# Scores by query of the first two or three steps of the last three layers, and their maxima, moved into the MLP before

## What is computed

```python
x = L0(x, ctx)      # two cross attentions of 16 heads x 128, then MLP 0 (gelu)
x = L1(x, ctx)      # LN, cross attention of 16 heads x 16, then MLP 1 (LN, gelu)
x = L2(ctx, x)      # keys and values from [ctx, x] (512 keys), 16 heads x 16, then MLP 2 (rms)
x = L3(x, ctx)      # 32 query heads x 8 on 8 key heads, additive mask, layer norm at the end
# each attention: softmax(q k^T) v, so each query row needs the maximum of its 256 or 512 scores
```

## Time and profile before

| | us |
|---|---|
| median of three runs (1248.19 to 1248.85) | 1248.57 |
| the profiled execution | 1249.79 |
| its span, first to last instruction | 1248.4 |
| PE / PE weight load / DVE / ACT / POOL busy | 1203.5 / 1029.8 / 888.7 / 779.8 / 598.9 |
| handoff MLP 0 to layer 1, 1 to 2, 2 to 3 | at 695, 850 and 1052 |

### The profile page before, as it was taken

The page is one execution under the profiler, slowest core; times in us unless marked ns, Lnnn a source line. Parts: engine busy times, 40 slices in busy tenths (PEclk is TensorE's granted clock), DMA queues, the critical chain, the costliest instruction groups (busy, mean ns, idle before and its releaser), DMA issues.

```text
span 1248.4 us, 27144 instructions
## 1 busy us (share of the span) xinstructions
PE 1203.5 (96%) x9940; PEld 1029.8 (82%) x9940; DVE 888.7 (71%) x2304; ACT 779.8 (62%) x1889; POOL 598.9 (48%) x966
## 2 busy tenths in 40 slices
PE   8999999999999999999989899999999899999997
PEld 7999999999999999999978665786675577666664
DVE  5887877779887777778865787537788464666764
ACT  4876666668876566666874566645676654555553
POOL 3784555548875555454862443504444131324333
PEclk9999999999999999999999999999999999999999
DMA  5540100013431001001420220122222012121100
GB/s 170 153 141 31 35 26 27 27 39 107 142 100 35 27 26 35 27 27 28 126 74 27 81 81 28 51 69 74 84 68 70 10 60 64 54 70 42 40 12 18
DMA packets 56820, 75.03 MB, mean 60 GB/s; under 512 B 11312, under 2 KB 30576, under 8 KB 56688
## 3 DMA queue, kind: packets, MB, share of 16 engines
q1 hardware_dynamic: 51568, 72.75, 19.1%
q0 software_dynamic: 5120, 0.56, 0.3%
HBM read 49.46 MB, written 1.05 MB: 40 GB/s over the span
## 4 chain that ended last, share of the span: by engine, by line
PE 80%; DVE 7%; issue 5%; ACT 4%; POOL 2%; DMA 1%; ACTq 0%; DVEq 0%; POOLq 0%
PE bank L125 19%; PE bank L127 18%; PE bank L126 18%; PE bank L2052 5%; PE bank L771 4%; PE bank L1999 3%; PE bank L2009 3%; PE bank L1985 2%; PE bank L2010 2%; PE bank L1981 1%; ACT PT L2126 1%; DMA Q<-rows 1%; PE bank L178 1%; PE bank L713 1%; PE bank L1736 1%
## 5 line engine op out<-in xcount | busy, mean ns | idle before, releaser
L1095 POOL TENSOR_SCALAR E<-E,rl 128x256 f32<-128x256 f32 x256 | 243.6, 962 | 210.2 <-DVE rl L980 210.2
L2126 ACT ACTIVATE PT<-bank 128x512 f32<-128x512 f32 x320 | 173.5, 594 | 92.6 <-PE bank L2010 56.0
L846 ACT ACTIVATE QTh<-bank,bqs 128x256 fp32r<-128x256 f32 x128 | 60.8, 475 | 156.3 <-PE bank L127 156.2
L2207 DVE CUSTOM_DVE_ANT_0 Em<-bank,M 128x256 bf16<-128x256 f32 x256 | 95.1, 420 | 53.8 <-PE bank L1985 22.3
L856 ACT ACTIVATE E<-bank,nm 128x257 f32<-128x257 f32 x256 | 119.5, 481 | 1.2 <-DVE nm L950 1.0
L984 DVE TENSOR_TENSOR PTl<-bank,PTh 128x512 fp32r<-128x512 f32 x128 | 88.0, 688 | 27.3 <-ACT PTh L868 26.8
L957 DVE SCALAR_TENSOR_TENSOR QTl<-bank,bqs,QTh 128x256 fp32r<-128x256 f32 x128 | 61.6, 481 | 64.0 <-ACT KT L847 63.2
L868 ACT CAST PTh<-bank 128x512 fp32r<-128x512 f32 x128 | 75.2, 588 | 43.2 <-PE bank L771 43.2
L2201 DVE TENSOR_REDUCE nm<-bank 128x1 f32<-128x512 f32 x128 | 83.3, 685 | 23.5 <-PE bank L1981 22.3
L950 DVE TENSOR_REDUCE nm<-bank 128x1 f32<-128x257 f32 x256 | 95.5, 414 | 3.6 <-PE bank L127 3.6
L1999 PE MATMUL bank<-Q,K 51*128 51x256 f32 (+1 forms) x640 | 85.2, 315 | 4.9 <-DMA Q<-rows 2.4
(11 more groups left out here) (438 smaller groups left out, 4382.2 us busy)
## 6 DMA issues: line engine op xcount, KB each, us to landing
stage<-in_wts SPq DMA_DIRECT2D x99, 256.0 KB, 3.3
U<-in_vrows SPq DMA_DIRECT2D x64, 256.0 KB, 2.7
K<-stage SPq DMA_DIRECT2D x48, 128.0 KB
Q<-stage SPq DMA_DIRECT2D x48, 128.0 KB
K<-stage SPq DMA_DIRECT2D x48, 64.0 KB
Q<-stage SPq DMA_DIRECT2D x48, 64.0 KB
K<-xh SPq DMA_DIRECT2D x16, 128.0 KB, 3.0
Q<-rows POOLq DMA_DIRECT2D x96, 4.0 KB, 1.7
```

The costliest lines, as they stand in the source:

```text
L1095: m = pool.tensor_scalar(s.E[:, i % 3, t, 0:256], s.E[:, i % 3, t, 0:256], s.rl[:, r, t:t + 1], None, ALU.mult)
L2126: act.activation(s.PT[i % s.NPT][:, 2 * u:2 * u + 2, :].rearrange("p a b -> p (a b)"), s.STB[y][:], ACT.Exp).then_inc(S["t_ex"])
L2207: dve.tensor_tensor_reduce(out=s.Em[:, (2 * i + e) % 4], in0=bank[:, e * 256:e * 256 + 256], in1=s.M3[:, j, e, :], scale=-1.0, scalar=3.4e ...
```

## The change

Steps 0 and 1 of layer 1, and 0 to 2 of layers 2 and 3, have their scores by query and maxima formed in steps 14 and 15, or 13 to 15, of the MLP before, in banks 6, 3 and 4. Batch 0's preparation comes a step earlier, layer 2 turns and projects x in bank 6, the fillers stay in the later of the first five steps only, and one-off work moves: the ones of K on GpSimd from before step 0 to step 3, the Exp table from step 3 to step 0, the ones of Q and V on ScalarE from steps 0 to 6 to steps 3 to 8. The tiles nm and Em are taken before the MLP.

```diff
@@ mlp_pe, mlp_dve, in each step i
+        for n in nxt.early(i):
+            heads_early_pe(c, nxt, n)
...
+        for n in nxt.early(i):
+            for k in nxt.in_step(n):
+                heads_maxima(c, nxt, k)
@@ tables
-              8: ["stats"], 9: ["norm"], 10: ["turn", "scale"], 11: ["th", "tl", "res"], 12: ["q0", "q1", "qh", "ql"],
-              13: ["q_out", "stats+"], 14: ["norm+"], 16: ["turn+", "scale+"]},
+              8: ["stats"], 9: ["norm", "turn", "scale"], 10: ["th", "tl", "res"], 11: ["q0", "q1", "qh", "ql"],
+              12: ["q_out", "stats+"], 13: ["norm+"], 16: ["turn+", "scale+"]},
...
-              9: ["turn", "th", "tl", "res"], 10: ["q0", "q1", "qh", "ql"], 11: ["q_out", "x0", "x1", "xh", "xl"],
-              12: ["x_out", "v2", "v3", "vb"]},
+              8: ["turn", "th", "tl", "res"], 9: ["q0", "q1", "qh", "ql"], 10: ["q_out", "x0", "x1", "xh", "xl"],
+              11: ["x_out", "v2", "v3", "vb"]},
-          3: {3: ["mask"], 6: ["k0", "kh", "kl"], 7: ["v0", "v1", "va", "k_out"], 8: ["maskparts"],
-              9: ["turn", "th", "tl", "res"], 10: ["q0", "q1", "qh", "ql"], 11: ["q_out"]}}
+          3: {3: ["mask"], 6: ["k0", "kh", "kl"], 7: ["v0", "v1", "va", "k_out"],
+              8: ["turn", "th", "tl", "res"], 9: ["q0", "q1", "qh", "ql"], 10: ["q_out", "maskparts"]}}
+EARLY = {1: {14: 0, 15: 1}, 2: {13: 0, 14: 1, 15: 2}, 3: {13: 0, 14: 1, 15: 2}}
...
-ONES_AT = {1: {0: ("q", 1, 0), 1: ("q", 1, 1), 2: ("v", 1, 0), 4: ("q", 2, 0), 5: ("q", 2, 1), 6: ("v", 2, 0)},
-           2: {1: ("q", 1, 0), 2: ("q", 1, 1), 3: ("v", 1, 0), 4: ("v", 1, 1)}, 3: {1: ("v", 1, 0)}}
+ONES_AT = {1: {3: ("v", 1, 0), 4: ("q", 1, 0), 5: ("q", 1, 1), 6: ("q", 2, 0), 7: ("q", 2, 1), 8: ("v", 2, 0)},
+           2: {5: ("q", 1, 0), 6: ("q", 1, 1), 7: ("v", 1, 0), 8: ("v", 1, 1)}, 3: {5: ("v", 1, 0)}}
@@ class Heads
+        self.E, self.EB = len(EARLY[l]), [c.B[6], *c.B[3:5]]
...
+    def query_bank(self, n):
+        return self.EB[n % 3] if n < self.WD * self.E else self.SB[n % 3]
+    def asked(self, n):
+        return self.in_step(n) if n >= self.E else ()
@@ heads_by_query, now a function of its own
+    if n < 3:
+        w.wait_ge(S["m_hf"], 4 * (l - 1) + 3)
+        w.wait_ge(S["m_x"], 4 * (l - 1) + 2)
+    elif first <= n < first + 3:
+        w.wait_ge(S["m_gelu"], 16 * l)
+        w.wait_ge(S["t_mx"], s.o["mx"] + first * k)
+    else:
+        w.wait_ge(S["t_mx"], s.o["mx"] + (n - 2) * k)
@@ heads_pe: keep_busy
-        if n < s.L:
-
-            w.wait_ge(S["m_x"], 4 * (l - 1) + 2)
+        if s.E <= n < s.L:
+
+            w.wait_ge(S["t_mx"], s.o["mx"] + s.WD * s.E * (2 if l == 3 else 1))
             ones(s.STB[1], {1: 4, 2: 4, 3: 6}[l])
@@ heads_act
-        if n == s.L - 2:
+        if n == 0:
             w.wait_ge(S["neghalf"], 1)
             act.activation(c.tiny[:], c.neghalf, ACT.Exp)
@@ heads_pool
-    ones_keys(c, s, 1)
     for n in range(s.steps()):
         for g in s.turns_at(n - 1):
             maxima_rows(g)
+        if n == 3:
+            ones_keys(c, s, 1)
         for g in s.turns_at(n):
             maxima_parts(g)
```

More of the change, by code:

```diff
@@ L1257, in take_first @@
         self.qbs = sb("qbs", [128, 2], F32, self.above)
+        self.nm = self.main("nm", [128, 4, self.G, 2])
+        if self.l == 3:
+            self.Em = self.main("Em", [128, 4, 256], BF16)
     def take_rest(self, c):
@@ L1281, in x_bank, with early @@
     def x_bank(self, b):
-        return self.MB if b and self.l == 2 else self.PB
+        return self.PB if self.l != 2 else self.MB if b else self.EB[0]
+    def query_bank(self, n):
+        return self.EB[n % 3] if n < self.WD * self.E else self.SB[n % 3]
+    def early(self, i):
+        return [EARLY[self.l][i]] if i in EARLY[self.l] else []
+    def asked(self, n):
+        return self.in_step(n) if n >= self.E else ()
     def all(self, n):
@@ L1548, in heads_prep_pe @@
                 w.wait_ge(S["h_y"], s.pk(0) + 1)
+        elif l == 2:
+            w.wait_ge(S["m_hf"], 4 * (l - 1) + 3)
         else:
@@ L1955, in heads_sp, with heads_ready, heads_by_query, heads_early_pe @@
         w.wait_ge(S["st_out1"], 48)
+def heads_ready(c, s, b):
+    S, w, l = c.S, c.pe_w, s.l
+    for x in "qk":
+        w.wait_ge(S["dma_h" + x], 64 * s.spreads(b + 1))
+        w.wait_ge(S["dma_l" + x], 32 * s.spreads(b + 1))
+    if l == 2:
+        w.wait_ge(S["dma_hx"], 64 * (b + 1))
+        w.wait_ge(S["dma_lx"], 32 * (b + 1))
+    if l != 3:
+        w.wait_ge(S[f"dma_mask{b % 2}"], 32 * (2 * (l - 1) + b // 2 + 1))
+def heads_by_query(c, s, n, e):
+    S, pe, w, l = c.S, c.pe, c.pe_w, s.l
+    p, u, y = s.unit(n)
+    q, r = p % s.P, p // s.P % s.NR
+    at = s.at(q, y, s.R)
+    bank, first, k = s.query_bank(n), s.WD * s.E, 2 if l == 3 else 1
+    if n < 3:
+        w.wait_ge(S["m_hf"], 4 * (l - 1) + 3)
+        w.wait_ge(S["m_x"], 4 * (l - 1) + 2)
[4 more added lines that the diff above has]
+        w.wait_ge(S["t_mx"], s.o["mx"] + (n - 2) * k)
+    if l == 2:
+        pe.matmul(bank[:], s.Q[r][at, q, u * 128:u * 128 + 128], s.K[r][at, q, :], start=True, stop=True
+                  ).then_inc(S["t_s"])
+        return
+    z = pe.matmul(bank[:, 256 * e:256 * e + 256], s.Q[r][at, q // s.blocks, 128 * e:128 * e + 128],
+                  s.K[r][at, q // s.rp, :], start=True, stop=True)
+    if e == 1:
+        z.then_inc(S["t_s"])
+def heads_early_pe(c, s, n):
+    if n == 0:
+        heads_ready(c, s, 0)
+    for e in (range(1) if s.l == 2 else range(2)):
+        for k in s.in_step(n):
+            heads_by_query(c, s, k, e)
 def heads_pe(c, s, nxt):
@@ L1960, in heads_pe @@
     nh, nkt = s.nh, s.nkt
[L1962 to L1988, removed]
     def by_key(n, e):
@@ L2013, in fours @@
     def fours(n):
[L2015 to L2018, removed]
+        if 0 < n < s.T and n % s.TB == 0:
+            heads_ready(c, s, n // s.TB)
         for e in (range(1) if l == 2 else range(2)):
-            for k in s.in_step(n):
-                by_query(k, (e,))
+            for k in s.asked(n):
+                heads_by_query(c, s, k, e)
         for e in range(2):
@@ L2183, in heads_act, with heads_maxima @@
         close_act(c, s)
-def heads_dve(c, s, nxt):
[L2187 to L2209, removed]
+def heads_maxima(c, s, n):
+    S, dve, w, l = c.S, c.dve, c.dve_w, s.l
+    p, u, y = s.unit(n)
+    i = 2 * p + y
+    g, h = i // s.G, i % s.G
+    nm, bank = s.nm[:, g % 4, h, :], s.query_bank(n)
+    w.wait_ge(S["t_np"], s.o["g"] + g - 3)
+    w.wait_ge(S["t_s"], s.o["s"] + n + 1)
+    if l == 1:
+        dve.tensor_reduce(nm, bank[:].rearrange("p (a b) -> p a b", a=2), AX.X, ALU.max, negate=True
+                          ).then_inc(S["t_mx"])
+    elif l == 2:
+        dve.tensor_reduce(nm[:, u:u + 1], bank[:], AX.X, ALU.max, negate=True).then_inc(S["t_mx"])
+    else:
+        j = i // s.nh % 2
+        w.wait_ge(S[f"ld_m3{j}"], 16 * (i // s.nh // 2 + 1))
+        for e in range(2):
+            w.wait_ge(S["t_mx"], s.o["mx"] + 2 * i + e - 3)
+            dve.tensor_tensor_reduce(out=s.Em[:, (2 * i + e) % 4], in0=bank[:, e * 256:e * 256 + 256],
+                                     in1=s.M3[:, j, e, :], scale=-1.0, scalar=3.4e38, op0=ALU.add,
+                                     op1=ALU.min, accum_out=nm[:, e:e + 1]).then_inc(S["t_mx"])
@@ L2211, in heads_dve @@
+def heads_dve(c, s, nxt):
+    w, l = c.dve_w, s.l
     mlp_end(c, w, l - 1)
     for n in range(s.steps()):
-        for k in s.in_step(n)[:s.WD - 1]:
-            maxima(k)
+        for k in s.asked(n)[:s.WD - 1]:
+            heads_maxima(c, s, k)
         for b, x in s.preps(n - 1):
@@ L2223, in heads_dve @@
             piece_dve(c, k)
-        for k in s.in_step(n)[s.WD - 1:]:
-            maxima(k)
+        for k in s.asked(n)[s.WD - 1:]:
+            heads_maxima(c, s, k)
     if l == 3:
```

9 lines of the change are left out of this document (2 added, 7 removed).

## The result

| | before | after |
|---|---|---|
| median of the runs, us | 1248.71 (4 runs, 1248.19 to 1250.28) | 1260.1 (4 runs, 1257.87 to 1264.12) |
| ratio, 95% interval | 1 | 1.0088 [1.0076, 1.0100] |
| profiled execution / its span | 1249.79 / 1248.4 | 1261.03 / 1259.5 |
| granted clock, mean over the span | 0.990 | 0.980 |
| time at the lower clock in the profiled execution | 25.7 | 52.5 |

The change makes the kernel 0.9% slower, 11 us. The forecast had the sign, its 4.95 us were less than half of it, and 1260.1 lies above the range.

A forecast was written before the change was run, and what follows sets the result against it. TensorE was taken as the bound; layer 1 +0.8, layer 2 +1.7 and layer 3 +2.45 gave +4.95 us on a median of 1248.57, so 1253.5. The forecast's own range was 1250.5 to 1257.5; 1246.0 to 1257.0 leaves out under 2 in 10.

The forecast's parts named there:

- What bounds it: Whole kernel: TensorE is the bound, so a microsecond counts only if TensorE loses or saves it; moved waits count nothing.
- Layer 1: Handoff from MLP 0 and layer 1: late maxima and K's later fill against fillers gone, +0.8 us.
- (c): Layer 1: k of batch 1 still waits for residual and scale; layer 2: waits of 1.3 for residual, 1.3 for parts.
- rival 3: Handoff to layer 1: the clock falls there too, a low stretch of 3.4 us costs 1.7, 1255.2; chance 0.15.
- (d): Layer 1: later K fill delays step 8, +0.8 (-1.5 to +2.5); layer 2: casts in steps 5 to 8, +0.8.
- Layer 2: MLP 1 and layer 2: 0.9 for casts in the MLP, 0 up to step 5, 0.8 after it, +1.7 us.
- (a): Layer 2: two casts on ScalarE meet in one MLP step and delay gelu, +0.9 us, bounds 0 and 1.05.
- (b): Layer 2: early scores in MLP steps 13 to 15, with maxima between low parts on VectorE, +1.4 us.
- Layer 3: MLP 2 and layer 3: q0 0.25 later, and a gap of 4.1 us drops the clock, +2.2; +2.45 us.
- Rival 1: All three layers: fills of K and Exp table done before TensorE needs them, -3.2 us, 1245.4; chance 0.22.
- Rival 2: Whole kernel: waits come but the clock holds and casts in steps 5 to 8 are covered, +1.95, 1250.5; chance 0.21.
- Rival 4: MLPs: a late spread or maximum holds the early scores and TensorE, another 2 to 4 us, 1256.5; chance 0.04.

The follow-up runs named there:

- a1: Changed kernel with GpSimd's fill of K behind the first group's parts (layers 1, 3) or second group's (layer 2): 1258.67 us, 1.0071 to the kernel before.
- a4: Changed kernel with the Exp table loaded in step 3 again: 1257.85 us, 1.0063 to the kernel before.
- c4: b1 plus fillers dropped from the early steps: 1252.68 us, 1.0017 to the kernel before.
- a3: Changed kernel with the casts of ones on ScalarE back where they were: 1263.14 us, 1.0098 to the kernel before.
- d1: b1 plus the fill of K in step 3 and fillers only in steps 3 and 4: 1256.8 us, 1.0055 to the kernel before.
- c1: b2 with layer 2's fill of K cut into two halves, in steps 2 and 4: 1246.69 us, 0.9964 to the kernel before.
- c3: b1 plus the fill of K in step 3: 1254.19 us, 1.0032 to the kernel before.
- d2: b1 plus fillers only in steps 3 and 4 and the Exp table at step 0: 1258.43 us, 1.0058 to the kernel before.
- b1: Kernel before plus only early scores, their maxima and earlier preparation; fillers, casts, Exp table and fills of K unmoved: 1253.23 us, 1.0023 to the kernel before.
- b2: Changed kernel with all side edits rearranged: fill as in a1, Exp table in step 2, fillers numbered per step, casts spread: 1250.47 us, 1.0003 to the kernel before.
- a2: Changed kernel with the fillers of all five first steps back: 1256.2 us, 1.0059 to the kernel before.

## Why the prediction was wrong in size

**What bounds it: right.** TensorE is busy 176 of 184 us in layer 3 and 146.5 of 157 in layer 2, and of its waits 2.33 us (a1, layer 1) and 1.5 (a4, layer 3) came off where the work that they waited for was moved.

**Layer 1: the waits right, a fall of the clock missed, +0.8 in the sum, +2.6 measured** (720.68 against 717.40 at step 8, less the 0.69 that was there at the start). Normalised tokens, maxima before GL (+0.90 for +0.75) and k_out behind the fill came as forecast. Missed in (c) was a new fall of the clock: the fillers and scores that had stood in the gap ahead of k were only counted as filling, and without them the gap is 1.85 us and the clock low for 3.4 us. This is rival 3's event, and it came besides the forecast, not in its place. The Trainium skill (TensorE: Matmul & The Clock Gate, PE-mode transpose) says that transposes don't count as TensorE being busy in the way of other matmuls; the trace agrees with it only in so far as the clock fell, at 700.19, after a gap of 1.85 us with four transposes before it. That it was they is not shown: c4 has the same gap of 1.85 us and ran on at 1.00 from 697 to 704. In (d), q_out's issues ended at 718.2 for a forecast 716.3; the start, MLP 0 and that low stretch explain it. The wait of 2.33 us at step 8 came behind it, and the low stretch that begins at 713.8 (before: 712.3) lasts 10.2 us and not 6.8. The upper bound, +2.5, was near the measured value.

**Layer 2, (a), (b), (c): right.** MLP 1 +2.57 for 2.3, up to step 5 -1.41 for -1.4. **(d): the step that failed**, +0.8 for casts in steps 5 to 8, bounds 0 and 2.0, where +5.78 was measured from step 5 to the layer's end. Its price was that of ScalarE's work, and a fall of the clock was put at nothing. The clock is what costs most there, at 1.2 GHz for 13.7 us (4.9 of the 5.78), from 1.0 us behind the turn that had waited 1.37 us. For this gap, hardly longer than the 1.20 us of that in the earlier trace rows, the prediction counted 1.3 us in (c) and no fall, although it took the fall in layer 3 from that very row. In a3 and d1 the casts are gone from these steps and the low clock is not, for 10.2 us each; in c1, with casts of its own in steps 2 to 4 and 9, the wait is short (0.59 us) and the clock stays up. That the wait brings the fall is likely and not shown, since c3 waits 1.39 us and the clock stays up.

**Layer 3: right, by its sum** (2.45 for 2.44: MLP 2 +1.67, the rest +0.77). The gap is 4.13 for 4.1. The clock fell inside it, 1.7 us before its end, for 6.8 us: 5.1 at half clock behind the restart, where 4.4 were taken. The chain ahead of q0 was put at 3.25 us, though its five rows add up to 3.06 without any overlap; 3.24 were measured from the residual to q0, so part of that agreement is luck. What the table at step 0 costs in this handoff once the fillers are gone is 2.2 us by a4 and 4.3 by d2 (-1.43 to +2.91); 1.5 of it is the longer gap, and the low stretch grows from 3.4 to 6.8 and to 10.2 us.

**The sum as a whole.** It had one loss by the clock, 2.2 us. The bounds of its parts, added up, give 1247.3 to 1257.8 and not 1250.5 to 1257.5; 1260.1 is above both. From run to run of one and the same kernel the span grows by 0.32 us for each us at the lower clock (least squares about each kernel's mean, 177 runs; 0.23 to 0.43 within the groups of ten runs or more). The changed kernel is at the lower clock for 25 us more than the kernel before, by this price an estimated 8 us (6 to 11 with the price between 0.23 and 0.43). That leaves some 3 of the 11 us for work and waits. What they are is not shown: b1 costs 3 us too, but with its 9 us of fillers, and the same sum leaves -0.4 us for c4 and -1.0 for d1, which have the moved scores without them.

**Rivals.** Rival 1 (the one-off work off the path, 1245.4) did not happen here, but its two places matter: c1 takes the fill and the table off the path, with the fillers and casts placed anew as well, and ran at 1246.69. Rival 2 needed a clock that holds; b1 is its nearest run, at +0.23%. Rival 4 did not happen: TensorE shows no wait for a spread in an MLP.

## What to carry to other kernels

Count for each gap that a change makes on TensorE, even one of 1.4 us, a possible low stretch behind it, of 3 to 14 us at half speed where TensorE is the bound; by the estimate above this came to more here than all the waits together. Fillers look like waste in a profile, so ask of each which gap it covers before it goes: alone their removal cost nothing here (c4), and with a later fill or an earlier table load the two together cost 4 us (d1, d2, against b1). One-off work of 1 to 4 us on a helping engine belongs in a stretch where that engine waits anyway, in pieces if it must; ahead of the parts of a group that TensorE needs it cost waits of 1.4 to 2.3 us here (the changed kernel, a1, b2).

## What was not expected of the hardware

- The length of a gap alone does not say whether the clock falls. In layer 2, at the longest wait for a group's parts (the first group's in b1, c4 and d2, the third's in a1 and b2, else the second's): 1.37 us went with 13.7 us at the lower clock (after), 1.38 with 6.8 (a2), 1.47 with 13.7 (a4), 1.79 with 10.2 (d1), 2.06 and 3.16 with 10.2 (a1, a3), but 2.28, 2.76 and 2.77 with only 3.4 (b2, d2, c4), and 1.39 and 1.75 with none (c3, b1). In layer 3, ahead of q0, it went in order: no gap, no low stretch (a2, b1, c3); 2.63 us, 3.4 us (a4, c4, d1); 4.13 us, 6.8 us (after) or 10.2 (a1, a3, d2). The fall comes inside the gap (layer 3, after) or up to 1.5 us behind its end (layer 1, after). What else decides is open.
- The low stretches behind these gaps lasted 3.4, 6.8, 10.2 or 13.7 us, also while TensorE is busy without a gap: from 864 to 877 it was busy all of 13.00 us.
- Executions of one kernel differ by several us, with their low time: 1257.87 to 1264.12 over four of the changed kernel, 1246.39 to 1254.81 over 77 of the kernel before beside the experiments. Four are too few to say that the scatter grew.
